# Attention prologue moved among the last experts, a bank of its own for the last batch, and a values' product in two key blocks

## The chip, the cores and the metric

One core of one Trainium2 chip runs one program. The metric is the device time of one execution in microseconds (us), lower is better. In a trace, engines are PE (matrix products), DVE, ACT and POOL; PE loads weights as instructions of their own (PEld).

## What is computed

Four stages on x of 4 batches of 256 tokens and 128 features, each with a layer norm and a residual:

```python
x = x + xattn0(layernorm(x), ctx, ...)   # trilinear attention, context to query and query to context
x = x + experts(layernorm(x), Wg, W1, W2, W3)   # 8 experts, top 2, silu(x W1) * (x W2) W3
x = x + xattn1(layernorm(x), ctx, Wq, Wk, Wv, Wo, bo)   # 16 heads of 8, softmax over 256 keys
x = x + ffn1(layernorm(x), kernel, bias)   # scaled, rounded to float8, product, bfloat16 bias
```

The change touches the third stage, and the second where the third now reaches into it.

## The kernel before

Every engine has a hand-written order of instructions, and semaphores in the dictionary S join them: `then_inc` counts up, `wait_ge` holds the engine, and everything behind it, until the count is there. PSUM has eight banks bk[0] to bk[7] of 128 partitions by 512 fp32 numbers.

**Start.** `project_keys` (L1056) multiplies wk with ctxT, a half of the tokens at a time, into banks 2 and 3, after the values' projection (L1051) and just ahead of the experts; ACT copies the result over ctxT (L402). PE's wait for cv is at L1003.

**Experts.** 16 units (8 experts for each half of the tokens). PE: `up(n)` (12 products of 512 columns, lines 933 to 935, into banks 0 to 3), then `down(n - 2)` (L1110, into bank 4 or 5). ACT: `gates` (L409). DVE: `hidden` (L756) and `weigh(n - 2)` (L768), which adds the weighted result to xs. The first half of xs is complete after unit 7; its layer norm for the attention is `sum_moments` on DVE in unit 9, POOL's `deviation_and_shift` (lines 237 to 276), four `third_scaled` on ACT (L413) in units 10 and 11, `turn("ln3", ...)` on PE (L941) after down() of unit 12, `third_turned` on ACT (L427), and `project_queries(0)` (L1117) at the head of unit 13. ACT and DVE split the queries into a high and a low part (L432, L779).

**Attention.** 16 groups of 4 heads, m = 4 b + g for batch b. For a group, `pick_group` (L1127) spreads queries and keys of its heads over 32-row strips, ACT's `stacked` (L438) moves them to stk; `scores(m, r)` (L1144), one strip r at a time, gives head r's scores; DVE's `maxima` (L789) takes the row maxima into negm; `turn_maxima` (L1152) transposes these; DVE's `shifted` (L798) puts them into qa; `shifted_scores` (L1164) computes the scores once more, transposed, with the shift, into banks 3 to 6; ACT's `exps` (L446) writes probs; `outputs` (L1177) multiplies them with values and ones into bank 7; ACT's `o_copy` (L454) takes it to heads_out. Per batch, `turn_outputs` (L1186), DVE's `normalise` (L806, L808), `turn_normalised` (L1193), ACT's `turned_out` (L458), `output_layer` (L1199) and DVE's `add_attention` (L815) follow, spread over the groups of the next batch by `bank7_used` and `bank7_free`, which also hold what has to be read from bank 7 before outputs overwrites it. `keep_warm` (L947) are products of the identity with itself whose result nobody reads.

On PE a group runs: `turn_maxima(m)`, `bank7_used(m)`, `scores(m+1, 1)`, `pick_group(m+3)`, `shifted_scores(m)`, `scores(m+1, 2)`, `scores(m+1, 3)`, `bank7_free(m)`, `outputs(m-1)`, `scores(m+2, 0)`. On DVE: `maxima(m+1, 0)`, `shifted(m)`, `maxima(m+1, 1)`, extras, `maxima(m+1, 2)`, extras, `maxima(m+1, 3)`. In groups 0 and 1 the extras are the moments of the second half of xs (L563, L566), in group 13 both halves' `normalise`. The stretch between experts and groups is:

```python
down(UNITS - 2); scores(0, 0); scores(0, 1); down(UNITS - 1); pick_group(2)
scores(0, 2); keep_warm(7, 4); scores(0, 3); keep_warm(7, 3); scores(1, 0)
```

SP issues loads and the three stores alone; no DMA is touched.

## Time and profile before

| | us |
|---|---|
| median of 3 runs | 216.92 |
| lowest, highest | 216.85, 217.7 |
| profiled execution, its own time | 218.05 |
| span of its trace | 216.3 |

The profile says 87% busy for PE, 64% for DVE, 48% for ACT and 17% for POOL, and a mean granted clock of 0.945. A row of the timeline gives start and length; instructions of one line that follow each other are merged (xN), and square brackets say how long the engine was idle before and who released it. A row of the chain gives start, length and what the chain ran through. Matmul records overlap, so a merged length is a little longer than the share of the chain.

### The profile page before, as it was taken

Reading aid. Unit: us, or ns where it says so; the run is one execution under the profiler, and the core shown is the slowest. Engines: PE = TensorE matmul, PEld = TensorE weight load, DVE = VectorE, ACT = ScalarE, POOL = GpSimd, SP = SyncE. Lnnn points to the kernel's source line nnn. Section 1 sums busy time; section 2 is a strip of 40 time slices with the busy share of each in tenths; the row PEclk is TensorE's granted clock in tenths of the full one; section 3 lists DMA queues with packets and bytes.
Section 4 is the critical chain, followed back from the end, with each engine's and each line's share of the span. In section 5 each row is a group of like instructions: output and inputs, shape, how many; then the busy total and the mean of one; then the engine's idle time right before and its main releaser. Section 6 shows DMA issues by size and latency. Waiting matters only on the chain.

```text
span 216.3 us, 3877 instructions
## 1 busy us (share of the span) xinstructions
PE 188.8 (87%) x1386; PEld 146.3 (68%) x1386; DVE 139.3 (64%) x404; ACT 103.9 (48%) x184; POOL 36.7 (17%) x52
## 2 busy tenths in 40 slices
PE   5599799999999999998999999799999998789221
PEld 4289498779798888996789886456666665554110
DVE  2559758666467647553546778477777876554684
ACT  2247467535422232533233146887577666345333
POOL 3623374624000000300000005200000000003400
PEclk9999999999999999999999999999999999655955
DMA  6992000000000000000000000000000000000002
GB/s 205 387 397 92 5 0 2 0 3 0 0 5 0 0 0 3 0 0 0 3 0 0 2 3 0 0 3 0 5 0 3 0 5 0 0 3 2 0 0 97
DMA packets 3330, 6.61 MB, mean 31 GB/s; under 512 B 880, under 2 KB 2160, under 8 KB 3056
## 3 DMA queue, kind: packets, MB, share of 16 engines
q1 hardware_dynamic: 1440, 5.51, 6.7%
q10 hardware_dynamic: 1872, 0.87, 1.4%
q8 instruction: 11, 0.18, 0.3%
q14 instruction: 7, 0.06, 0.1%
HBM read 5.84 MB, written 0.52 MB: 29 GB/s over the span
## 4 chain that ended last, share of the span: by engine, by line
PE 74%; DVE 11%; issue 5%; ACT 5%; ACTq 3%; POOL 1%; DVEq 0%
PE banks L1110 13%; PE bank L1144 9%; PE bank L1177 8%; PE bank L933 5%; PE bank L935 5%; PE bank L934 5%; DVE negm L789 4%; PE bank L947 3%; PE bank L1152 3%; PE banks L934 2%; PE banks L933 2%; PE banks L935 2%; ACTq L328 2%; PE bank L1186 2%; PE bank L1127 2%
## 5 line engine op out<-in xcount | busy, mean ns | idle before, releaser
L789 DVE TENSOR_REDUCE negm<-bank 128x2 f32<-128x512 f32 x64 | 43.0, 689 | 18.9 <-PE bank L1144 18.7
L446 ACT ACTIVATE raw<-banks 128x1024 f32<-128x1024 f32 x32 | 31.0, 1021 | 21.4 <-PE banks L1164 21.4
L409 ACT ACTIVATE att<-bank 128x512 f32<-128x512 f32 x32 | 19.1, 598 | 38.5 <-PE bank L935 25.6
L1144 PE MATMUL bank<-stk 32*128 32x256 f32 x128 | 29.9, 319 | 3.9 <-DVE negm L789 3.3
L1144 PEld LDWEIGHTS bank<-stk 32*128 32x128 f32 x128 | 19.4, 191 | 15.9 <-issue 12.8
L768 DVE SCALAR_TENSOR_TENSOR xs<-banks,rw,xs 128x128 f32<-128x128 f32 x64 | 18.0, 345 | 6.0 <-PE banks L1110 5.8
L1110 PEld LDWEIGHTS banks<-raw,attT 128*128 128x128 f32 x176 | 21.3, 191 | 0.9
L1110 PE MATMUL banks<-raw,attT 128*128 128x128 f32 x176 | 21.5, 275 | 0.0
L1177 PE MATMUL bank<-raw,vones 128*32 128x256 f32 x256 | 19.9, 433 | 1.1 <-DVE ao L808 1.0
L933 PE MATMUL bank<-xT,w 128*128 128x512 f32 x48 | 20.6, 428 | 0.0
L237 POOL TENSOR_SCALAR vpe<-mv 128x4 f32<-128x4 f32 (+1 forms) x9 | 2.4, 266 | 97.7 <-DVE mv L566 97.6
L935 PE MATMUL bank<-xT,w 128*128 128x512 f32 x48 | 18.8, 392 | 0.0
L934 PE MATMUL bank<-xT,w 128*128 128x512 f32 x48 | 18.8, 391 | 0.0
L438 ACT ACTIVATE stk<-bank,const 128x512 fp32r<-128x512 f32 x16 | 11.2, 699 | 8.8 <-PE bank L1127 8.8
L756 DVE TENSOR_TENSOR attT<-att,bank 128x512 f32<-128x512 f32 x11 | 7.5, 683 | 10.3 <-ACT att L409 10.3
L1164 PE MATMUL banks<-qa,stk 32*128 32x256 f32 x128 | 13.5, 335 | 0.5 <-DVE qa L798 0.5
L1177 PEld LDWEIGHTS bank<-raw,vones 128*32 128x32 f32 x256 | 8.4, 119 | 6.8 <-issue 1.9
L756 DVE TENSOR_TENSOR attT<-att,banks 128x512 f32<-128x512 f32 x11 | 7.6, 688 | 7.2 <-ACT att L409 7.2
L263 POOL TENSOR_TENSOR w<-raw,w 128x512 fp32r<-128x512 f32 x8 | 10.1, 1286 | 6.6 <-ACT w L341 5.2
L933 PEld LDWEIGHTS bank<-xT,w 128*128 128x128 f32 x48 | 9.0, 188 | 2.7 <-DVE xT L697 0.5
L1164 PEld LDWEIGHTS banks<-qa,stk 32*128 32x128 f32 x128 | 10.0, 198 | 0.9 <-DVE qa L798 0.9
L935 PEld LDWEIGHTS bank<-xT,w 128*128 128x128 f32 x48 | 9.0, 188 | 2.1
(194 smaller groups left out, 347.6 us busy)
## 6 DMA issues: line engine op xcount, KB each, us to landing
raw<-in_w SPq DMA_DIRECT2D x1, 2048.0 KB, 10.7
raw<-in_w SPq DMA_DIRECT2D x1, 1024.0 KB, 8.5
xs<-in_x SPq DMA_DIRECT2D x2, 256.0 KB, 3.2
ctxT<-in_ctxT SPq DMA_DIRECT2D x1, 512.0 KB, 5.3
ctx<-in_ctx SPq DMA_DIRECT2D x1, 512.0 KB, 7.4
wl<-in_wl SPq DMA_DIRECT2D x1, 256.0 KB, 7.6
picks<-in_sel ACTq DMA_DIRECT2D x1, 256.0 KB, 10.9
out<-cT SPq DMA_DIRECT2D x1, 256.0 KB, 2.1
```

Of the source, the lines that this page charges most:

```text
L409: act.activation(silus[:, k, :], bk[2 * k][:, :], ACT.Silu).then_inc(S["silu_s"], 1)
L446: act.activation(probs[:, m % 2, 2 * r:2 * r + 2, :, :].rearrange("p h k q -> p (h k q)"), pair[r][:, :], ACT.Exp, scale=ATT_SCALE).then_i ...
L756: dve.tensor_tensor(hid[n % 3][:, k, :], silus[:, k, :], bk[2 * k + 1][:, :], ALU.mult)\
L768: ins = dve.scalar_tensor_tensor(xs[:, tile, :], bk[4 + n % 2][:, t * P:(t + 1) * P], rw[:, tile, e:e + 1], xs[:, tile, :], ALU.mult, ALU.add)
L789: dve.tensor_reduce(negm[:, m % 2, :, c0:c0 + 1].rearrange("p t c -> p (t c)"), bk[score_bank(m, r)][:, :].rearrange("p (t k) -> p t k", t ...
L933: pe.matmul(out, w[0], x[0], start=start, stop=False)
L934: pe.matmul(out, w[0], x[1], start=False, stop=False)
L935: return pe.matmul(out, w[1], x[0], start=False, stop=stop)
L1110: ins = pe.matmul(bk[4 + p][:, rows], hid[n % 3][:, k, rows], w3raw[:, e, k * P:(k + 1) * P], start=t == 0 and k == 0, stop=t == TPH - 1 a ...
L1144: ins = pe.matmul(bk[score_bank(m, r)][:, t * SEQ:(t + 1) * SEQ], stk[rows, m % G, t * P:(t + 1) * P], stk[rows, m % G, SEQ:2 * SEQ], star ...
L1164: ins = pe.matmul(bk[3 + j][:, t * SEQ:(t + 1) * SEQ], stk[rows, g, SEQ + t * P:SEQ + (t + 1) * P], qa[rows, m % 2, :], start=True, stop=T ...
L1177: ins = pe.matmul(bk[bank][QUAD * j:QUAD * (j + 1), SEQ:2 * SEQ], vones[:, t, (m % G) * HPG + j, :], probs[:, m % 2, j, t, :], start=t == ...
```

## The change

- The first key product goes between context_to_query(1) and the wait for cv; both keys land in kraw, which shares x3T's memory, and ACT copies the first ahead of the values.
- The turn, queries and selections of the first groups go one unit earlier, and behind up(); group 0's scores stand around down() in units 14 and 15, all in bank 6, DVE's maxima around weigh(). The last down() goes into group 0, into bank 7; the one before it uses bank 0. DVE's last two weigh() go into group 0.
- ACT's third_scaled of unit 10 and 11 join in unit 10; those of group 2 go ahead of its exponentials. DVE's moments of groups 0 and 1 join in group 1.
- 15 keep_warm products go from units and group 0, four come into the last group.
- outputs is split by key block, with scores(m+2, 0) between the two.
- Batch 2's turns, layer and normalising use bank 0; its second turn goes behind the values' product of group 13, its output layer into group 14.

```diff
@@ -31,7 +31,7 @@
 SHIFT_ROW = 24
-WARMED = (0, 1, 2, 2 * G - 1, 3 * G - 1)
+WARMED = (1, 2, 2 * G - 1, 3 * G - 1)
@@ -140,6 +140,7 @@
 x3T = sb("x3T", [P, TOK])
+kraw = x3T
@@ -179,11 +180,17 @@
 def score_bank(m, r):
     if m == 0:
-        return 2 - r % 2
+        return 6
...
 def turn_bank(b, t):
-    return 0 if t == 0 and b >= BATCH - 2 else 7
+    return 0 if b == BATCH - 2 or (t == 0 and b == BATCH - 1) else 7
...
+def layer_bank(b):
+    return 0 if b == BATCH - 2 else 7
...
+def y_bank(n):
+    return {UNITS - 2: 0, UNITS - 1: 7}.get(n, 4 + n % 2)
@@ -277,7 +284,7 @@
     pool.wait_ge(S["k_hi"], 1)
-    pool.tensor_tensor(kx[:, 1, :], ctxT[:, :], plain(kx[:, 0, :]), ALU.subtract).then_inc(S["k_lo"], 1)
+    pool.tensor_tensor(kx[:, 1, :], kraw[:, :], plain(kx[:, 0, :]), ALU.subtract).then_inc(S["k_lo"], 1)
...
     def values(b, first):
@@ -394,12 +401,15 @@
+    def keys_out(h):
+        act.wait_ge(S["k_ps"], h + 1)
+        act.copy(kraw[:, h * HALF:(h + 1) * HALF], bk[2 + h][:, :]).then_inc(S["k_out"], 1)
...
+    keys_out(0)
...
     normed_hi(0)
-    for h in range(2):
-        act.wait_ge(S["k_ps"], h + 1)
-        act.copy(ctxT[:, h * HALF:(h + 1) * HALF], bk[2 + h][:, :]).then_inc(S["k_out"], 1)
+    keys_out(1)
     def gates(n, first):
@@ -455,7 +465,7 @@
     def turned_out(b):
         act.wait_ge(S["aoT_ps"], b + 1)
-        act.copy(aoT[:, :], bk[7][:, 0:SEQ]).then_inc(S["aoT_ev"], 1)
+        act.copy(aoT[:, :], bk[layer_bank(b)][:, 0:SEQ]).then_inc(S["aoT_ev"], 1)
     def act_group(m):
@@ -465,27 +475,27 @@
             turned_out(b - 1)
+        if m == 2:
+            for t in range(*HALVES[1]):
+                third_scaled(t)
...
         if m >= 1:
-            o_copy(m - 1, 0 if m == GROUPS - 1 else 7)
+            o_copy(m - 1)
...
             stacked(m + 3)
-        if m == 2:
-            for t in range(*HALVES[1]):
-                third_scaled(t)
...
             logits_out(1)
-        if n == UNITS - 3:
+        gates(n, n == 0)
+        if n == UNITS - 4:
             queries_hi(0)
-        if n >= UNITS - 2:
-            stacked(n - UNITS + 2, 7)
-        gates(n, n == 0)
+        if n >= UNITS - 3:
+            stacked(n - UNITS + 3, 7)
         if n == 2:
-            act.copy(kx[:, 0, :], ctxT[:, :]).then_inc(S["k_hi"], 1)
+            act.copy(kx[:, 0, :], kraw[:, :]).then_inc(S["k_hi"], 1)
@@ -493,13 +503,12 @@
             gap_tanh(n // 5)
-        if n in (E + 2, E + 3):
-            for k in range(HB):
-                third_scaled(HB * (n - E - 2) + k)
-        if n == E + 4:
+        if n == E + 2:
+            for t in range(*HALVES[0]):
+                third_scaled(t)
+        if n == E + 3:
...
     act.activation(spare[:, :], const[:, C_ZERO:C_ZERO + 1], ACT.Exp)
-    stacked(2)
@@ -765,7 +774,7 @@
             tile = h * TPH + t
-            ins = dve.scalar_tensor_tensor(xs[:, tile, :], bk[4 + n % 2][:, t * P:(t + 1) * P],
+            ins = dve.scalar_tensor_tensor(xs[:, tile, :], bk[y_bank(n)][:, t * P:(t + 1) * P],
@@ -813,7 +822,7 @@
         dve.tensor_tensor(xs[:, tiles, :], xs[:, tiles, :],
-                          bk[7][:, 0:SEQ].rearrange("p (t d) -> p t d", t=TPB), ALU.add)\
+                          bk[layer_bank(b)][:, 0:SEQ].rearrange("p (t d) -> p t d", t=TPB), ALU.add)\
...
     def dve_group(m):
@@ -824,6 +833,8 @@
             maxima(m + 1, 1)
+        if m == 0:
+            weigh(UNITS - 2)
@@ -834,15 +845,18 @@
             maxima(m + 1, 2)
-        if m in (0, 1):
-            sum_moments((TPH + TPB * m, TPH + TPB * (m + 1)))
+        if m == 0:
+            weigh(UNITS - 1)
+        if m == 1:
+            sum_moments(HALVES[1])
+        if more:
+            maxima(m + 1, 3)
...
             normalise(b - 1, 1)
-        if more:
-            maxima(m + 1, 3)
+        if m == GROUPS - 2:
+            add_attention(b - 1, slice(TPB * (b - 1), TPB * b))
...
             moments(4, CHUNKS[0], lambda t: dve.wait_ge(S["x3_s"], t // TPB + 1))
-            add_attention(b - 1, slice(TPB * (b - 1), TPB * b))
@@ -853,17 +867,18 @@
             routing(n // 5)
-        if n == UNITS - 3:
+        if n == UNITS - 4:
             queries_lo(0)
+        if n == UNITS - 2:
+            dve.wait_ge(S["setup"], 1)
+        if n >= UNITS - 2:
+            maxima(0, 2 * (n - UNITS + 2))
...
             weigh(n - 2)
+        if n >= UNITS - 2:
+            maxima(0, 2 * (n - UNITS + 2) + 1)
...
             sum_moments(HALVES[0])
-    weigh(UNITS - 2)
-    dve.wait_ge(S["setup"], 1)
-    maxima(0, 0, 1)
-    weigh(UNITS - 1)
-    maxima(0, 2, 3)
@@ -1000,6 +1015,12 @@
     context_to_query(1)
+    def project_keys(h):
+        ins = pe.matmul(bk[2 + h][:, :], wk[:, :], ctxT[:, h * HALF:(h + 1) * HALF], start=True, stop=True)
+        ins.then_inc(S["k_ps"], 1)
...
+    pe.wait_ge(S["ld_att"], 7 * 16)
+    project_keys(0)
@@ -1053,14 +1074,7 @@
-    def project_keys(h):
-        if h == 0:
-            pe.wait_ge(S["aT_ev2"], BATCH - 1)
-        ins = pe.matmul(bk[2 + h][:, :], wk[:, :], ctxT[:, h * HALF:(h + 1) * HALF], start=True, stop=True)
-        ins.then_inc(S["k_ps"], 1)
...
-    for h in range(2):
-        project_keys(h)
+    project_keys(1)
     def logits(h):
@@ -1099,15 +1113,17 @@
     def down(n):
-        e, p = n % E, n % 2
+        e = n % E
...
         pe.wait_ge(S["hid_s"], HB * (n + 1))
-        if n > 1:
+        if 1 < n < UNITS - 2:
             pe.wait_ge(S["y_w"], n - 1)
+        if n == UNITS - 1:
+            pe.wait_ge(S["stack_s"], 3)
...
             for k in range(HB):
-                ins = pe.matmul(bk[4 + p][:, rows], hid[n % 3][:, k, rows], w3raw[:, e, k * P:(k + 1) * P],
+                ins = pe.matmul(bk[y_bank(n)][:, rows], hid[n % 3][:, k, rows], w3raw[:, e, k * P:(k + 1) * P],
@@ -1121,6 +1137,8 @@
         pe.wait_ge(S["stack_s"], m)
+        if m == 3:
+            pe.wait_ge(S["y_w"], UNITS - 1)
@@ -1131,14 +1149,14 @@
     def scores(m, r):
         pe.wait_ge(S["stack_s"], m + 1)
-        if r == 0 and m > 0:
+        if m == 0:
+            pe.wait_ge(S["s1_max"], r)
+        elif r == 0:
             pe.wait_ge(S["s1_max"], 4 * m - 1)
-        elif r == 2 and m > 0:
+        elif r == 2:
             pe.wait_ge(S["qa_s"], m)
-        elif r == 3 or (r == 1 and m > 0):
+        else:
             pe.wait_ge(S["s1_max"], 4 * m + (r + 1) // 2)
-        elif r == 2:
-            pe.wait_ge(S["s1_max"], 1)
@@ -1155,6 +1173,8 @@
     def shifted_scores(m):
         pe.wait_ge(S["qa_s"], m + 1)
+        if m == 0:
+            pe.wait_ge(S["y_w"], UNITS - 2)
@@ -1167,17 +1187,18 @@
-    def outputs(m, bank=7):
+    def outputs(m, bank=7, blocks=range(TPB)):
...
             pe.wait_ge(S["o_ev"], m)
-        for j in range(HPG):
-            for t in range(TPB):
+        for t in blocks:
+            for j in range(HPG):
...
                                 start=t == 0, stop=t == TPB - 1, tile_position=(0, QUAD * j))
-        ins.then_inc(S["pv_ps"], 1)
+        if blocks[-1] == TPB - 1:
+            ins.then_inc(S["pv_ps"], 1)
     def turn_outputs(b, t):
@@ -1190,13 +1211,13 @@
     def turn_normalised(b):
...
         for t in range(TPB):
-            ins = pe.transpose(bk[7][:, t * P:(t + 1) * P], ao[:, t, :], ident)
+            ins = pe.transpose(bk[layer_bank(b)][:, t * P:(t + 1) * P], ao[:, t, :], ident)
...
     def output_layer(b):
...
         for t in range(TPB):
-            ins = pe.matmul(bk[7][:, t * P:(t + 1) * P], aoT[:, t * P:(t + 1) * P], wo[:, :],
+            ins = pe.matmul(bk[layer_bank(b)][:, t * P:(t + 1) * P], aoT[:, t * P:(t + 1) * P], wo[:, :],
@@ -1207,36 +1228,39 @@
             turn("ln3", "x3T_ps", 7, 1)
+        if m == 1:
+            pe.wait_ge(S["y_w"], UNITS)
...
             project_queries(1)
-        if g == 0 and b >= 2:
+        if g == 0 and 2 <= b:
             output_layer(b - 2)
+        if m == 3 * G + 1:
+            pe.wait_ge(S["stack_s"], GROUPS)
         if b >= 1 and g == 1:
-            if b == BATCH - 1:
-                pe.wait_ge(S["stack_s"], GROUPS)
             turn_outputs(b - 1, 0)
-            if b == BATCH - 1:
-                turn_outputs(b - 1, 1)
...
         if m in TURNED_AT:
+            pe.wait_ge(S["ao_s"], TPB * b)
...
     def bank7_free(m):
         b, g = m // G, m % G
+        if m == 1:
+            pe.wait_ge(S["y_w"], UNITS)
...
             pe.wait_ge(S["x3_s"], b - 1)
-        if b >= 1 and g == 1:
-            pe.wait_ge(S["ao_s"], TPB * (b - 1) + (1 if b < BATCH - 1 else TPB))
+        if 1 <= b < BATCH - 1 and g == 1:
+            pe.wait_ge(S["ao_s"], TPB * (b - 1) + 1)
...
             pe.wait_ge(S["ao_s"], TPB * b)
-        if m in TURNED_AT:
+        if 1 <= b < BATCH - 1 and g == 3:
...
     def pe_group(m):
@@ -1246,25 +1270,31 @@
             scores(m + 1, 1)
-        if m + 3 < GROUPS:
+        if 0 < m < GROUPS - 3:
...
         shifted_scores(m)
-        if final:
-            pe.wait_ge(S["o_ev"], m - 1)
-            output_layer(BATCH - 2)
-            outputs(m - 1, 0)
+        if m == 0:
+            down(UNITS - 1)
...
             if m == 0:
-                keep_warm(7, 2)
+                pick_group(3)
             scores(m + 1, 3)
-        if m == 0:
-            keep_warm(7, 4)
-        if m >= 1 and not final:
+        if m >= 1:
             bank7_free(m)
-            outputs(m - 1)
+            outputs(m - 1, 7, (0,))
...
             scores(m + 2, 0)
+        if m >= 1:
+            outputs(m - 1, 7, (1,))
+        if m == 3 * G + 1:
+            pe.wait_ge(S["ao_s"], TPB * (BATCH - 2) + 1)
+            turn_outputs(BATCH - 2, 1)
+        if m == 3 * G + 2:
+            pe.wait_ge(S["aoT_ev"], BATCH - 1)
+            output_layer(BATCH - 2)
+        if final:
+            keep_warm(2, 4)
@@ -1278,40 +1308,34 @@
             pe.wait_ge(S["xT_lo"], 2)
-        if n == UNITS - 3:
-            pe.wait_ge(S["route_s"], 18)
-            project_queries(0)
-        if n == UNITS - 2:
-            pe.wait_ge(S["pick_s"], 1)
-            pe.wait_ge(S["k_lo"], 1)
-        if n >= UNITS - 2:
-            pick_group(n - UNITS + 2, 7)
...
             logits_turned(1)
+        if n == UNITS - 5:
+            turn("ln3", "x3T_ps", 6, 0)
+        if n == UNITS - 4:
+            pe.wait_ge(S["route_s"], 18)
+            project_queries(0)
+        if n == UNITS - 3:
+            pe.wait_ge(S["pick_s"], 1)
+            pe.wait_ge(S["k_lo"], 1)
+        if n >= UNITS - 3:
+            pick_group(n - UNITS + 3, 7)
+        if n >= UNITS - 2:
+            scores(0, 2 * (n - UNITS + 2))
...
             logits(1)
-        if n == E + 4:
-            turn("ln3", "x3T_ps", 6, 0)
+        if n >= UNITS - 2:
+            scores(0, 2 * (n - UNITS + 2) + 1)
+    pe.wait_ge(S["hid_s"], HB * UNITS)
+    scores(1, 0)
     down(UNITS - 2)
-    pe.wait_ge(S["hid_s"], HB * UNITS)
-    for r in range(2):
-        scores(0, r)
-    down(UNITS - 1)
-    pick_group(2)
-    scores(0, 2)
-    pe.wait_ge(S["stack_s"], 2)
-    keep_warm(7, 4)
-    scores(0, 3)
-    keep_warm(7, 3)
-    scores(1, 0)
-    pe.wait_ge(S["setup"], 1)
...
     outputs(GROUPS - 1, 1)
+    pe.wait_ge(S["x3_s"], BATCH - 1)
     turn_outputs(BATCH - 1, 0)
-    pe.wait_ge(S["x3_s"], BATCH - 1)
...
     output_layer(BATCH - 1)
```

## Rows read from the trace of the kernel before

**Rows 1.** The page: its span, and the granted clock and DMA share in 40 slices.

```profile
span 216.3 us, 3877 instructions
PEclk9999999999999999999999999999999999655955
DMA  6992000000000000000000000000000000000002
```

**Rows 2.** The page's costliest groups (operation, shapes, busy, mean, idle before).

```profile
L789 DVE TENSOR_REDUCE negm<-bank 128x2 f32<-128x512 f32 x64 | 43.0, 689 | 18.9 <-PE bank L1144 18.7
L446 ACT ACTIVATE raw<-banks 128x1024 f32<-128x1024 f32 x32 | 31.0, 1021 | 21.4 <-PE banks L1164 21.4
```

**Rows 3.** Timeline of an attention group: start, length, engine and line, idle before.

```profile
157.76 1.09 PE L1177 MATMUL bank<-raw,vones 128*32 128x256 f32 x16
158.78 0.50 PE L1144 MATMUL bank<-stk 32*128 32x256 f32 x2
159.22 0.44 PE L1152 MATMUL bank<-const,negm 128*128 128x128 f32 x2
159.22 0.69 ACT L438 ACTIVATE stk<-bank,const 128x512 fp32r<-128x512 f32 x1
159.49 0.61 PE L1199 MATMUL bank<-wo,aoT 128*128 128x128 f32 x4
160.16 0.35 PE L1144 MATMUL bank<-stk 32*128 32x256 f32 x1
161.51 0.47 PE L1144 MATMUL bank<-stk 32*128 32x256 f32 x2 [0.26 <-DVE negm L789]
```

**Rows 4.** Timeline and chain of waits around the key products.

```profile
23.98 0.60 PE L1005 MATMUL banks<-const,cv 128*4 128x128 f32 x4 [1.31 <-DVE cv L638]
...
37.90 0.69 DVE L697 TENSOR_TENSOR xT<-banks,xT 128x512 fp32r<-128x512 f32 x1
...
38.10 0.86 PE banks L1059 x2
```

**Rows 5.** Timeline of experts 12 and 13.

```profile
97.34 1.13 DVE L768 SCALAR_TENSOR_TENSOR xs<-banks,rw,xs 128x128 f32<-128x128 f32 x4 [0.47 <-PE banks L1110]
98.50 1.10 PE L1117 MATMUL bank<-x3T,wq 128*128 128x512 f32 x2 [0.77 <-ACT x3T L427]
...
104.61 0.47 PE L1127 MATMUL bank<-qx,pick 32*128 32x256 f32 x2 [0.46 <-DVE qx L779]
```

**Rows 6.** Groups by line on PE from 120 to 129 us; chain of waits there.

```profile
L947 PE MATMUL bank<-const 128*128 128x128 f32 x34 | 5.2, 287 | 0.0
...
120.58 1.09 PE bank L947 x8
```

**Rows 7.** Timelines of DVE, POOL and PE, and the chain, up to group 3.

```profile
131.03 0.30 DVE L566 BATCH_NORM_AGGREGATE mv<-stats 128x2 f32<-128x6 f32 x2
...
133.26 0.20 POOL L276 TENSOR_TENSOR nmr<-nmr,rstd 128x4 f32<-128x4 f32 x1
...
136.96 1.53 ACT xn L413 x4
...
137.49 1.38 PE L941 MATMUL bank<-const,xn 128*128 128x128 f32 x4 [0.90 <-ACT xn L413]
```

**Rows 8.** Timeline and chain of waits of the last batch.

```profile
180.95 1.07 PE L1186 MATMUL bank<-const,heads_out 128*128 128x128 f32 x8 [0.36 <-issue]
184.80 1.19 PE L1177 MATMUL bank<-raw,vones 128*32 128x256 f32 x16 [1.02 <-DVE ao L808]
...
190.12 1.89 PE bank L1177 x16
195.10 3.67 PE bank L1177 x32
```

**Rows 9.** Stretches: PE, PEld, DVE, ACT, POOL busy (instructions), PEclk, DMA share, GB/s.

```profile
134.50:138.00 3.50, 2.60 (x24) 1.31 (x23) 2.07 (x4) 3.50 (x8) 0.31 (x1) 1.00 0.00 0
182.00:185.50 3.50, 1.85 (x29) 1.27 (x30) 2.80 (x7) 1.94 (x2) 0.00 (x0) 1.00 0.00 0
```

## The prediction, made before the change was run

> **What bounds the kernel now.** I read the page first: busy times, slices and PEclk. The granted clock is full for 34 of 40 slices and falls near the end [rows 1]. Then the chain of waits, which shows TensorE nearly everywhere, and last the timelines of the places where the chain names something other than a dense PE stream.
>
> Two regimes. Through the experts (39 to 117 us) PE runs without a gap. In the attention groups one group takes some 4.15 us, in a ring. The second scores product of group m+1 starts at 160.16, its maxima on DVE take 0.69 [rows 2], the fourth product starts at 161.51 [rows 3], and then PE alone: that product (0.47), the values' product (from 157.76 to 158.78 in the group before, 1.02), the next first scores (158.78 to 159.22, 0.44), the maxima's transposes (0.37 of chain time) and one filler on bank 7 (from 159.49, 0.45 of chain time) [rows 3]. From 160.16 to 161.51 is 1.35, most of it work. So PE's own work is about 3.7 of 4.15, and what is merely reordered inside the ring brings little. The reader should look for what is outside it:
>
> - Keys and start of the experts: PE idles 1.31 before the row of maxima at 23.98, while both key products lie at 37.24 to 38.96, just ahead of the experts, which could start when DVE's low half is written, at 37.90 + 0.69 = 38.59 [rows 4].
> - Experts 12 and 13: PE stands 0.77 for the copy of x3T and 0.46 for the queries' low half [rows 5].
> - Groups 0 and 1: between 120 and 129 PE runs 34 keep-warm products, 5.2 us busy in that row [rows 6], in the places where it would wait.
> - Group 3: the second half's turn waits for four scalings on ACT and ends at 138.87 [rows 7]. The transpose of the maxima ended at 136.59.
> - Last batch: the values' product of group 12 waits 1.02 for normalising on DVE, since both halves were turned ahead of it and one of them is in its bank. Then the granted clock falls: the same 16 instructions of the values' product take 1.19, then 1.89, and the last 32 take 3.67 [rows 8], against 1.02 before. In the 3.5 us around the stall PE was busy 1.85; in group 3's stall 2.60 of 3.5, and the clock stayed [rows 9].
>
> **The sum, part by part** (chain time; minus is saved).
>
> 1. First key product (0.86) moves into the 1.31 hole at 22.7. Its cover is the wait for cv; without it, it would cost 0.86. It also moves the wait for the attention weights forward; the DMA row shows the last traffic in the fourth slice of 5.4 us, so by 21.6 [rows 1], before the hole. ACT's copy of it comes ahead of the values' copies, in idle time. The experts then start at 38.64 and not 38.96, DVE being late next: **-0.3**.
>
> 2. Turn, queries and selection one expert earlier, and behind up() instead of ahead of it: ACT's copies and DVE's subtraction pass under down() and the next up(). The two idles (0.77, 0.46) and the slow start of L1117 (1.10 for what L1059 does in 0.86) [rows 4, 5] go: **-1.45**. The four scalings now stand together on ACT in expert 10 and delay the next gate by some 0.2; the hidden layer has more slack than that, so nothing.
>
> 3. From expert 14 to group 3's second scores product (138.86). Keep-warms: 34 records fall to 4, which is 30 x 0.136 = **-4.1** (8 of them take 1.09 on the chain) [rows 6]. The last down() moves from ahead of group 0's third scores into group 0: neutral by itself. Added: eight more places where row-tiled products stand alone between full-array ones. What such a switch costs no row isolates. The nearest rows: a pair of scores takes 0.50 behind the values' product and 0.47 elsewhere [rows 3], and a turn or a selection behind down() overlaps its end or not, by up to 0.2. I take 0.1 each, between the two: **+0.8** (0 to 1.6). Overlap lost in group 0, whose second and third scores and selection shared PE with the shifted scores: **+0.75** (bounds 0 and 1.4, three pairs of 0.47 standing alone). New wait: DVE now does both last weigh() (1.13 each [rows 5]) inside group 0, between its maxima. The fourth maxima of group 1 ends about 5.9 + 0.7 after group 0's transposes begin, PE is done at 5.4: **+1.2** (0 to 1.9). In group 1 the four moments (two pairs of 0.6) stand together ahead of the fourth maxima, and turn_maxima(2) waits: **+0.75** (0 to 1.2). Who waits behind it on PE is the whole queue. Group 3: the scalings run ahead of group 2's exponentials, not behind them. They wait for POOL, which needs 133.46 - 131.33 = 2.1 behind the moments [rows 7], and push the exponentials (two of 1.02 [rows 2]) by 1.0; o_copy(1) follows them and PE waits some 0.9 for it, where it waited 1.9 before: **-0.9** (0 to -1.9). Rest of my timeline +0.35. Together **-1.1** (-3 to +0.8). Of the DVE moments' delay nothing else comes free: group 2 hides it.
>
> 4. The ring, groups 4 to 12. Splitting the values' product puts the next first scores 0.48 earlier, so DVE's first maxima no longer hold the second scores: they begin 0.06 behind the filler's end (159.49 + 0.61), where back-to-back groups overlap by 0.07 (158.78 against 157.76 + 1.09), so 0.13 is that wait. Against it stands a second switch, 0.1 and a little. And o_copy, hence stacked(m+3), now ends some 0.4 later; stacked ends at 159.91 [rows 3] with PE's selection just behind 160.16, so the selection slips by some 0.2 into the hole of 0.26 that follows (idle of the row at 161.51). Per group -0.1 to +0.15; I take 0, over nine groups -0.9 to +1.4: **0**. Here the row shows weights of L1144 loading only once the values' product is through: its first matmul and load begin together at 158.78, and two need 0.50 where 0.47 is the rule [rows 3]. The Trainium skill (TensorE: Matmul & The Clock Gate, Part 3, "The mechanism") says a weight load overlaps running matmuls only where the row group differs. The values' product fills all 128 rows, so by it each extra block is an exposed load, which speaks against this split, and over 14 groups the sum would be some 1.7 worse than mine.
>
> 5. Last batch, from group 13's transposes (180.95 - 0.36 - 0.37 = 180.22) to the end of the last values' product (195.10 + 3.67 = 198.77): 18.55 [rows 8]. After, at full clock, from X: transposes 0.37; wait for stacked(15), longer than the 0.36 by the later o_copy, 0.88; four transposes 0.5; to the fourth scores 1.35; 0.47; half values 0.51; wait for the third maxima behind one normalising 0.27; scores 0.43; 0.51; other four transposes 0.5: X+5.8. Before it was 6.5 with the stall. Then DVE, which has nothing else, normalises the second half (0.55, about half of the 1.02 that two of them held PE) ahead of the first maxima (0.69) + 0.15: second scores at X+7.25; +1.35; 0.47; values 1.02; output layer 0.45: X+10.55. Then 0.37, qa and shifted scores 1.05 (an estimate, below the 1.35 of a ring, which has more in it), two exponentials 1.94, values 1.02 behind the last: X+15.15. **-3.4**. At full clock both ways the old order would be shorter by 0.8; nearly all of the gain is the clock, which I take to stay up since the longest PE hole is now about 0.9 with 2.3 us busy in 3.5, as in group 3's case that kept it.
>
> 6. Behind this, DVE and POOL work on the final layer stays as it was: their slack in the last groups shrinks. 0.
>
> Sum: -0.3 - 1.45 - 1.1 - 0 - 3.4 = **-6.3**. The profiled execution took 218.05 (span 216.3, 1.75 around it) and would take 211.8. It lies 1.1 above the median of 216.92; part of that may be how long the low clock lasted. Against the median: 216.92 - 6.3 = 210.6.
>
> **Rivals.**
>
> B. The clock falls in the last batch all the same. For: little of groups 13 and 14 is values' product, and it once fell there. Against: no hole of 1 us. Price: the pieces at half clock against those at full, 0.87 for each values' product, 0.3 for scores, 0.25 for transposes, and 1.8 at the end, 4.2: **214.8**.
>
> C. The clock falls in groups 0 to 3, slower. Place: turn_maxima(1), waiting 1.2 for DVE with the keep-warms gone, then 0.75 and 0.9 in the next two. A ring's 3.7 of PE work becomes by the ratios of rows 8 (1.89 to 1.02) about 6.3: +2.2 a group. It decides from the third group on, since 6.3 / 2.2 = 2.9. With five groups at half clock: **221.6** (216.92 - 6.3 + 11). Against: at 21.5 to 25 and in group 3 the clock survived holes over 1 us [rows 7, 9].
>
> D. The split's second switch costs PE its 0.12 in each group, and the earlier maxima bring nothing, PE being the bound: 14 x 0.12 = 1.7 more: **212.3**. For: the rows of a ring [rows 3]. Against: the 0.13 that the second scores wait there. The rule of the Trainium skill's TensorE page named in 4 leads here. A kindred rival is that selections wait on stacked() by more than the hole hides, 0.2 x 9 = 1.8, the same time.
>
> E. It does not do what it says: groups 0 to 2 are bound by DVE (weigh, moments), so that removed keep-warms only become waits. Term 3 is then +0.8 and with B the sum is -0.35: **216.6**.
>
> **Chances.** Forecast 0.53, B 0.17, D 0.16, C 0.09, E 0.05. The range of A is 210.6 with -1.9 / +1.9 from terms 3 and 4; to D and B it reaches 215.2, below it 207.8. About 0.5% (1.1 us) is what a measurement of this kernel tells from no change. Faster 0.86, same 0.05, slower 0.09.
>
> **What would show it.** Right: L1059's first product at 22.7; up(0) at 38.6; no idle ahead of L1117 and L1127 in the experts; turn_maxima(1) near 125.3 behind a DVE wait; group 3's second scores at 136; steady rings of 4.15; PEclk 9 until the last slices; values' product of 1.02 in groups 13 and 14, split in two of 0.5. Wrong: PEclk below 9 in slices 22 to 34, rings of 4.3 or more, a stall on stk ahead of L1127, or DVE as releaser of L1152 in every group.

## The result, and the profile after

The changed kernel takes 227.41 us in the median of 4 runs (224.15 to 247.13), the kernel before 217.17. By the comparison, which leaves disturbed runs out, the ratio is 1.037 with a 95% interval of 1.028 to 1.046: slower. The spread of the changed kernel is itself a finding: over its four runs the mean granted clock went from 0.898 (span 222.3) down to 0.766 (span 245.3). The profiled execution took 228.54, span 226.8.

The page of the changed kernel, span and granted clock in 40 slices; before, the clock was full up to slice 34 [rows 1]:

```profile
span 226.8 us, 3850 instructions
PEclk9999999999999999999998555599999995556955
```

The clock is now low twice before the tail: from 123.2 to 147.1 and from 188.0 to 208.5. PE's timeline where it first falls (start, length, engine and line, idle before and its releaser), and two stretches of the windows (length, PE busy and four other engines' busy time, PEclk, DMA share, GB/s):

```profile
121.83 0.47 PE L1162 MATMUL bank<-stk 32*128 32x256 f32 x2 [0.40 <-DVE negm L798]
123.37 0.69 PE L1170 MATMUL bank<-const,negm 128*128 128x128 f32 x2 [1.07 <-DVE negm L798]
...
119.70:123.20 3.50, 2.20 (x18) 1.70 (x16) 2.22 (x7) 1.50 (x2) 0.00 (x0) 1.00 0.01 2
130.00:137.00 7.00, 7.00 (x46) 4.43 (x44) 3.10 (x5) 4.52 (x9) 2.96 (x4) 0.50 0.00 0
```

turn_maxima(1) (L1170) comes at 123.37, 4.5 earlier than before, but behind a hole of 1.07 us in which PE waits for DVE's maxima, and the clock falls in that hole. From 130 to 137 PE shows no idle time at all, at half clock. The start of turn_maxima(m), read from each trace, makes a table by group:

| stretch, us | before | after |
|---|---|---|
| start of turn_maxima(1) | 127.9 | 123.4 |
| groups 1 to 4 | 18.7 | 26.5 |
| groups 5 to 12 | 33.6 | 37.1 |
| group 13's transposes to the last values' product's end | 18.6 | 22.3 |
| from there to the span's end | 17.5 | 17.6 |

That is -4.5 + 7.8 + 3.5 + 3.7 + 0.1, the 10.5 between the spans but for rounding. Groups 5 to 12, the third line, are at full clock, where a group takes 4.54 to 4.76 in place of 4.14 to 4.36 [rows 3]. One such group:

```profile
149.88 0.44 PE L1170 MATMUL bank<-const,negm 128*128 128x128 f32 x2
150.02 0.37 ACT L464 COPY heads_out<-bank 128x256 f32<-128x256 f32 x1 [0.67 <-PE bank L1197]
150.53 0.63 PE L1207 MATMUL bank<-const,heads_out 128*128 128x128 f32 x4 [0.22 <-ACT heads_out L464]
151.09 0.38 PE L1162 MATMUL bank<-stk 32*128 32x256 f32 x1
...
152.47 0.47 PE L1162 MATMUL bank<-stk 32*128 32x256 f32 x2 [0.38 <-DVE negm L798]
152.87 0.64 PE L1197 MATMUL bank<-raw,vones 128*32 128x256 f32 x8
153.56 0.47 PE L1162 MATMUL bank<-stk 32*128 32x256 f32 x2
153.95 0.64 PE L1197 MATMUL bank<-raw,vones 128*32 128x256 f32 x8
154.52 0.44 PE L1170 MATMUL bank<-const,negm 128*128 128x128 f32 x2
```

Two things are new. The filler (L1207; the products that bank7_used puts behind the transposes) waits for ACT's o_copy (L464): it begins 0.65 behind the transposes of the maxima, 0.27 before (159.22 to 159.49 [rows 3]). And from the fourth scores (152.47) to the next transposes (154.52) is 2.05, where it was 1.85 before (161.51 to 163.36).

### The profile page after: what moved, and what is told of

Its sections match the earlier page's. It is cut to its first block, busy times and chain, and to the rows that moved or that the text cites. A ratio compares the mean times of both kernels' runs of the same rounds, so it can differ in the third digit from the quotient of the medians.

```text
span 226.8 us, 3850 instructions
## 1 busy us (share of the span) xinstructions
PE 200.6 (88%) x1364; PEld 147.1 (65%) x1364; DVE 140.3 (62%) x404; ACT 104.4 (46%) x184; POOL 36.8 (16%) x52
## 4 chain that ended last, share of the span: by engine, by line
PE 73%; DVE 13%; issue 5%; ACT 3%; DMA 3%; POOL 1%; SPq 1%; DVEq 0%; ACTq 0%
PE banks L1126 11%; PE bank L1197 11%; PE bank L1162 10%; PE bank L948 5%; PE bank L950 5%; PE bank L949 5%; DVE negm L798 4%; DMA ctx<-in_ctx 3%; PE bank L962 2%; PE bank L1207 2%; PE banks L948 2%; PE banks L949 2%; PE banks L950 2%; PE bank L1126 2%; PE banks L1184 2%
## 5 line engine op out<-in xcount | busy, mean ns | idle before, releaser
L798 DVE TENSOR_REDUCE negm<-bank 128x2 f32<-128x512 f32 x60 | 40.3, 689 | 21.7 <-PE bank L1162 21.1
L1162 PE MATMUL bank<-stk 32*128 32x256 f32 x120 | 32.4, 364 | 3.8 <-DVE negm L798 3.5
L1162 PEld LDWEIGHTS bank<-stk 32*128 32x128 f32 x120 | 21.8, 228 | 17.9 <-issue 16.9
L1197 PE MATMUL bank<-raw,vones 128*32 128x256 f32 x256 | 25.5, 488 | 0.0
L777 DVE SCALAR_TENSOR_TENSOR xs<-banks,rw,xs 128x128 f32<-128x128 f32 x56 | 15.8, 345 | 7.8 <-PE banks L1126 7.7
L1126 PEld LDWEIGHTS banks<-raw,attT 128*128 128x128 f32 x160 | 19.2, 192 | 1.2 <-issue 0.5
L1126 PE MATMUL banks<-raw,attT 128*128 128x128 f32 x160 | 19.7, 276 | 0.0
L1184 PE MATMUL banks<-qa,stk 32*128 32x256 f32 x128 | 16.0, 380 | 0.6 <-DVE qa L807 0.5
L464 ACT COPY heads_out<-bank 128x256 f32<-128x256 f32 x16 | 6.0, 373 | 16.0 <-PE bank L1197 16.0
L1184 PEld LDWEIGHTS banks<-qa,stk 32*128 32x128 f32 x128 | 12.0, 235 | 1.2 <-DVE qa L807 1.2
L270 POOL TENSOR_TENSOR w<-raw,w 128x512 fp32r<-128x512 f32 x8 | 10.2, 1291 | 6.6 <-ACT w L348 5.2
```

What stands on the lines that cost most here:

```text
L777: ins = dve.scalar_tensor_tensor(xs[:, tile, :], bk[y_bank(n)][:, t * P:(t + 1) * P], rw[:, tile, e:e + 1], xs[:, tile, :], ALU.mult, ALU.add)
L798: dve.tensor_reduce(negm[:, m % 2, :, c0:c0 + 1].rearrange("p t c -> p (t c)"), bk[score_bank(m, r)][:, :].rearrange("p (t k) -> p t k", t ...
L1126: ins = pe.matmul(bk[y_bank(n)][:, rows], hid[n % 3][:, k, rows], w3raw[:, e, k * P:(k + 1) * P], start=t == 0 and k == 0, stop=t == TPH - ...
L1162: ins = pe.matmul(bk[score_bank(m, r)][:, t * SEQ:(t + 1) * SEQ], stk[rows, m % G, t * P:(t + 1) * P], stk[rows, m % G, SEQ:2 * SEQ], star ...
L1184: ins = pe.matmul(bk[3 + j][:, t * SEQ:(t + 1) * SEQ], stk[rows, g, SEQ + t * P:SEQ + (t + 1) * P], qa[rows, m % 2, :], start=True, stop=T ...
L1197: ins = pe.matmul(bk[bank][QUAD * j:QUAD * (j + 1), SEQ:2 * SEQ], vones[:, t, (m % G) * HPG + j, :], probs[:, m % 2, j, t, :], start=t == ...
```

## Experiments

**Fill the hole (e1), join the product (e2), both (e3), split the old kernel (e4).**

e1, in pe_group, behind scores(m+2, 0):

```diff
+                if m == 0:
+                    pe.wait_ge(S["stack_s"], G)
+                    keep_warm(0, 8)
```

> The changed kernel with eight identity products (16 records) in bank 0 behind group 0's last product, once stacked(3) is read, so that PE works where it waited 1.07 us for the maxima. Theory 1 (the low clock of groups 1 to 4 comes from that hole): the clock stays full through groups 1 to 4, turn_maxima(1) comes at 123.4 to 123.7, groups 1 and 2 take 4.6 to 5 us in place of 6.6 and 6.8, and the time falls by 7 to 9 to 218 to 220. Rival (the clock falls for another reason, such as the smaller share of full-array work, or the last down() in group 0): it falls all the same within some 4 us, time within 2 of 227.

e2:

```diff
-                    outputs(m - 1, 7, (0,))
+                    outputs(m - 1)
                 if m + 2 < GROUPS:
                     scores(m + 2, 0)
-                if m >= 1:
-                    outputs(m - 1, 7, (1,))
```

> The changed kernel with the values' product in one piece again, ahead of scores(m+2, 0). Theory 2 (with the split, o_copy ends later than the transposes of the maxima, and bank7_used makes PE wait for it): groups at full clock return from 4.58 to 4.15, and nothing is idle ahead of the filler; the low clock in groups 1 to 4 stays; time 222 to 225. Rival (the second switch between row and column tiles costs the 0.43): the same 4.15, but the trace of the changed kernel would show no idle PE ahead of the filler. Rival (the ring grew by the later stacked(m+3)): also 4.15, idle ahead of L1145 there. Rival (DVE's order): stays 4.58.

e3 is e1 and e2 together:

```diff
-                    outputs(m - 1, 7, (0,))
+                    outputs(m - 1)
                 if m + 2 < GROUPS:
                     scores(m + 2, 0)
-                if m >= 1:
-                    outputs(m - 1, 7, (1,))
+                if m == 0:
+                    pe.wait_ge(S["stack_s"], G)
+                    keep_warm(0, 8)
```

> Both edits. Theories 1 and 2 add: about 227.4 - 8 - 5 = 214 to 215, below the kernel before, with groups 1 to 12 at 4.15 but for group 3. If the clock falls for another reason: as e2, 222 to 225.

e4, the kernel before with outputs() split as in the change:

```diff
-                    outputs(m - 1)
+                    outputs(m - 1, 7, (0,))
                 if m + 2 < GROUPS:
                     scores(m + 2, 0)
+                if m >= 1 and not final:
+                    outputs(m - 1, 7, (1,))
```

> The kernel before with the split alone. Theory 2: each group from 2 on takes 0.4 more, 12 x 0.43 = 5: 221 to 223, with the clock full until the last batch. Rival (the cost comes only together with the bank changes): within 1 of 217.

Measured, beside the kernel before at 217.83:

| | median (range), us | ratio to before |
|---|---|---|
| e1 fill | 217.76 (214.95 to 241.96) | 0.9985 [0.993, 1.004] |
| e2 whole | 211.63 (208.71 to 215.52) | medians 0.972, no interval |
| e3 both | 212.58 (210.02 to 225.03) | 0.971 [0.954, 0.987] |
| e4 split alone | 226.14 (225.69 to 228.09) | 1.040 [1.024, 1.056] |

e1's page, and the stretch around the former hole:

```profile
PEclk9859999999999999999999999999999999969955
...
119.70:123.20 3.50, 3.10 (x27) 2.67 (x26) 2.22 (x8) 2.44 (x3) 0.00 (x0) 1.00 0.01 2
130.00:137.00 7.00, 6.26 (x66) 4.16 (x65) 4.48 (x8) 5.93 (x11) 3.20 (x5) 1.00 0.00 0
```

The clock stays full there, groups 1 and 2 take 4.27 and 4.38 in place of 6.58 and 6.82, groups 1 to 4 together 18.7 as before the change, and the kernel is level with the one before. So it is this hole that costs the clock here: in both traces that have it open (the changed kernel, e2) the clock falls at or just behind it, and in all seven that have it filled (e1, e3, e5, e6, e9, e10, e12) it is full until 130 us at least. It isn't the only place: three of ten runs of e1 still took 238 to 242, and where the clock fell in these isn't known.

e2 is the surprise. I had expected 222 to 225, thinking that the low clock of groups 1 to 4 would stay as long as it did. It fell behind the same hole (which ends at 123.94), at 124.5, but came back after 6.8 us, not 23.9:

```profile
PEclk9999999999999999999999995999999999999855
...
175.19 1.07 PE L1197 MATMUL bank<-raw,vones 128*32 128x256 f32 x16
```

Its groups at full clock take 4.11 to 4.12 (4.36 with keep-warms), against 4.14 (4.36) before. All four runs of e2 lie below the lowest of the kernel before, 216.21. e4 says the same from the other side: the split alone costs the kernel before some 4%, 4.54 to 4.76 a group. That is above my 221 to 223, since the clock did not stay full: group 3 took 7.75 in place of 5.87. The hole ahead of the second half's turn was 1.19 us there, 0.90 before, and the clock fell at 139.5, 1.9 behind its end. e3 came out below its 214 to 215; eight products took more time than the hole had (group 0: 6.98 in place of 6.23), and in its profiled execution the clock fell at 133.2, in group 3's hole:

```profile
133.28 1.11 PE L956 MATMUL bank<-const,xn 128*128 128x128 f32 x4 [0.85 <-ACT heads_out L464]
```

**What in the split costs 0.43 a group (e5, e6, e9, e11).** Both e5 and e6 start from e1. e5 puts the filler, and its wait for o_copy, behind the second scores; e6 keeps the new order of the matmuls but nothing between the blocks:

```diff
# e5
-                if not final:
-                    bank7_used(m)
                 if more:
                     scores(m + 1, 1)
+                if not final:
+                    bank7_used(m)
# e6
                     outputs(m - 1, 7, (0,))
+                    outputs(m - 1, 7, (1,))
                 if m + 2 < GROUPS:
                     scores(m + 2, 0)
-                if m >= 1:
-                    outputs(m - 1, 7, (1,))
```

> The kernel of e1_warm (split kept, keep-warms in group 0's hole) with the filler on bank 7, and its wait for o_copy, behind scores(m+1, 1) instead of ahead of it. Theory 2 (of the 0.43 that a split ring takes more, some 0.3 is PE's wait for o_copy ahead of the filler, 0.12 the second switch): groups with the clock full take 4.2 to 4.3. Rival (it is the switches alone): 4.55 to 4.6 as in e1.

> The kernel of e1_warm with both key blocks in a row, so the new order of the 16 matmuls (key block outside, head inside) without the scores product in the middle. Theory 2: 4.12 to 4.15 a group at full clock, as with the old order. Rival (the order itself, or the four accumulations open at once, is slow): over 4.3.

e6 took 211.53, in one run, with 4.11 to 4.12 a group: the order itself is free. e5 said nothing on the ring: its clock fell at 130.2 and stayed low for 92 us, 246.11 in all (one run). I repeated it with the move in groups 5 to 12 only (e9):

```diff
+                late = G < m <= 3 * G
-                if not final:
+                if not final and not late:
                     bank7_used(m)
                 if more:
                     scores(m + 1, 1)
+                if late:
+                    bank7_used(m)
```

> As e5, but the filler and its wait for o_copy go behind scores(m+1, 1) only in groups 5 to 12, so that the early groups are those of e1_warm and the clock should be full where the rings are measured. Theory 2: those groups take 4.25 to 4.35 at full clock, against 4.58 in e1. Rival (the second switch alone makes the 0.43, o_copy nothing): 4.55 to 4.6.

Inconclusive again: low from 142.8 for 75 us, 239.07 (one run). What the two do show is that the clock falls without such a hole too: in the 8 us ahead of the fall PE's longest idle stretch was 0.50 in e5 and 0.40 in e9. e4's clock had been full there in its trace, so e11 makes the move on e4, in groups 6 to 12:

```diff
+                late = G + 1 < m <= 3 * G
-                if not final:
+                if not final and not late:
                     bank7_used(m)
                 if more:
                     scores(m + 1, 1)
+                if late:
+                    bank7_used(m)
```

> The kernel of e4_split_before (before with the split alone; its clock was full from 146 to 190 us) with the filler and its wait for o_copy behind scores(m+1, 1) in groups 6 to 12. Theory 2: at full clock these groups take 4.25 to 4.35, against 4.54 to 4.76 in e4. Rival (the second switch makes all of the 0.43): unchanged, 4.54 to 4.76. If the clock falls there, the test says nothing again.

Now (one run, 225.34) the clock was full from 147.7 to 192.1, and the groups took 4.28 to 4.30 (4.71 and 4.72 where keep-warms and a turn are among what moved) against 4.54 to 4.64 and 4.76 in e4. Its timeline, where ACT's copy (L454) no longer stands ahead of the second scores at 160.09:

```profile
159.71 0.44 PE L1152 MATMUL bank<-const,negm 128*128 128x128 f32 x2
159.85 0.37 ACT L454 COPY heads_out<-bank 128x256 f32<-128x256 f32 x1
160.09 0.49 PE L1144 MATMUL bank<-stk 32*128 32x256 f32 x2
```

So of the 0.43 some 0.3 is the wait for o_copy. The rest, 0.14 against the kernel before, is what stays when that wait is covered; the second switch of tiles is its likely cause, but no run isolates it. The changed kernel's own rows say the same: 0.3 more from the transposes to the fourth scores (2.59 against 2.29), 0.2 more from there on (2.05 against 1.85).

**Keep-warms and last batch alone, on the kernel before (e7, e8).** e7 takes the 15 keep-warm products out:

```diff
-WARMED = (0, 1, 2, 2 * G - 1, 3 * G - 1)
+WARMED = (1, 2, 2 * G - 1, 3 * G - 1)
...
-                    if m == 0:
-                        keep_warm(7, 2)
...
-                if m == 0:
-                    keep_warm(7, 4)
...
-            keep_warm(7, 4)
             scores(0, 3)
-            keep_warm(7, 3)
```

> The kernel before without its 15 keep-warm products between the last experts and group 1. Theory 1 (keep-warms hold the clock over holes there, and only that): the clock falls between 118 and 130 us in most executions, groups 1 to 3 take 6 us or more, time 222 to 228. Rival (the clock there hangs on the hole that weigh and moments make in the changed kernel, and the kernel before has none such): clock full, and since PE waits for DVE in the same places, time 215 to 217.

232.29 in the median (220.4 to 243.22), above my 222 to 228; the fastest of the four runs is 3.0 above the kernel before's median (217.35). Its trace, span 233.1, has the clock low from 122.1 for 10.2 us, and from 139.2 for 51. The holes are the one of 1.01 us shown here and group 3's of 0.90; the clock fell 2.1 and 2.2 behind their ends:

```profile
120.03 0.47 PE L1144 MATMUL bank<-stk 32*128 32x256 f32 x2 [1.01 <-DVE negm L789]
...
PEclk9889999999999999999995695555555569956955
...
160.00:175.00 15.00, 14.98 (x104) 10.12 (x104) 7.91 (x14) 8.12 (x11) 0.00 (x0) 0.50 0.00 1
```

So keep-warms were worth far more than the time they took. And the low clock can last in groups with an unsplit product too: the split isn't needed for it.

e8 makes the change's last batch on the kernel before: bank 0 for batch 2, its second turn behind group 13's product, the output layer in group 14, and DVE's order and the four keep-warm products of the last group as in the change. Two cuts of it:

```diff
                     turn_outputs(b - 1, 0)
-                    if b == BATCH - 1:
-                        turn_outputs(b - 1, 1)
...
+                if m == 3 * G + 1:
+                    pe.wait_ge(S["ao_s"], TPB * (BATCH - 2) + 1)
+                    turn_outputs(BATCH - 2, 1)
+                if m == 3 * G + 2:
+                    pe.wait_ge(S["aoT_ev"], BATCH - 1)
+                    output_layer(BATCH - 2)
+                if final:
+                    keep_warm(2, 4)
```

> The kernel before with the change's last batch alone (batch 2 through bank 0, its second turn behind group 13's values' product, four keep-warms in the last group). Step 5 of the prediction: from group 13's transposes of the maxima to the last values' product 15.2 in place of 18.55, clock full there, time 217.2 - 3.4 = 213.8 (213 to 215). Rival (the clock falls there all the same): 216 to 218.

215.11 in the median (213.43 to 217.8), ratio 0.988 [0.979, 0.997]: two runs at 213.4 and 213.7, as forecast, two at 216.5 and 217.8, as by the rival. The chain of waits in its trace, from group 13's transposes to the last values' product, to be held against [rows 8]:

```profile
179.79 0.37 PE bank L1156 x2
180.16 0.36 issue
180.52 0.63 PE bank L1190 x4
...
182.92 1.02 PE bank L1181 x16
...
188.14 1.02 PE bank L1181 x16
...
191.16 1.02 PE bank L1181 x16
192.18 1.09 PE bank L951 x8
193.27 1.09 PE bank L1181 x16
```

From 179.79 to 194.36 is 14.6, not 18.6, with every values' product at 1.02 to 1.09. This is a trace of the 213.7 run. Of the two runs above 216 only the mean clock is known, 0.934 and 0.956 against 0.970; where it fell isn't.

**A version that beats both (e10, e12).** e10 is e3 with four products, not eight, in group 0's hole. e12 adds two in group 13 and two in group 14, ahead of the waits there:

```diff
# e10, against e3
-                    keep_warm(0, 8)
+                    keep_warm(0, 4)
# e12, against e10
-WARMED = (1, 2, 2 * G - 1, 3 * G - 1)
+WARMED = (1, 2, 2 * G - 1, 3 * G - 1, 3 * G + 1, 3 * G + 2)
```

> The changed kernel with the values' product in one piece and four keep-warm products (8 records, 0.9 us) in group 0's hole of 1.07 us, half of those of e3, which made group 0 longer by 0.75. Theory: group 0 takes 6.25 as in e2, groups 1 and 2 4.3 and 4.0 as in e3, and the time is 209 to 212, the fastest of all. Rival (the clock falls as often as in e2 or e3, one hole later): 211 to 213, the same as e2.

> The kernel of e10_warm_four with two keep-warm products each in groups 13 and 14, ahead of PE's waits there for stacked(15) and for the normalised half. Theory (e10's slower executions, 215 against 209, are those in which the clock falls in the last batch, at 178 us in its trace): fewer of them, median 209 to 211. Rival (the clock falls as often): median 213 as e10, with at most 0.3 added for the products.

e10: 213.09 (209.03 to 215.08), 0.966 [0.959, 0.972]. Group 0 took 6.23, groups 1 and 2 4.33 and 4.02, as expected. The time was not: its trace, of a run of 214.98, has the clock falling at 177.9, in group 13, and three of six runs took about 215. e12: 209.18 (208.76 to 211.38), 0.966 [0.961, 0.970], all six runs within 2.6. Against e10's ratio it shows no gain; the median is 3.9 lower, and 8.2 below the kernel before (217.35). That the four products keep the clock in the last batch is likely (none of six runs near 215 in place of three, and the clock full there in its trace), but six runs each, on different chips, don't settle it. Its page:

```profile
span 207.0 us, 3867 instructions
PE 182.0 (88%) x1380; PEld 141.4 (68%) x1380; DVE 140.7 (68%) x404; ACT 103.6 (50%) x184; POOL 36.9 (18%) x52
PEclk9999999999999999999999999999999999999955
```

## Why the prediction was wrong

The prediction was -6.3 (210.6); the change gave +10. Two steps failed. One is step 4, the ring: it put the split of the values' product at 0 (-0.1 to +0.15 a group), and it costs 0.43 a group, mostly PE's wait for o_copy. The other is the clock, which step 3 put at nothing when it took out the keep-warms, and which step 5 took to stay up in the last batch; it was at half for 23.9 us from group 0's hole on and for 20.5 us from group 13 on. Between -6.3 and the +10.5 of the spans lie 16.8 us: 3.5 of these came in groups 5 to 12 (the split, at full clock), 6.2 before group 5 and 7.1 in the last batch (where the clock was low). By the prediction's steps:

1. **First key product: -0.3 predicted, -0.05 measured.** It went into the hole, whose idle shrank from 1.31 to 0.46. From the row of maxima to the experts' second matmul is 15.00 against 15.05 before. The key products had nearly all been under DVE's xT work already: the prediction took the start of the experts, 38.96, from the chain, which puts it at the modelled end of the key product, while PE's timeline of the kernel before has it at 38.64:

```profile
37.94 1.02 PE L1059 MATMUL banks<-ctxT,wk 128*128 128x512 f32 x2
38.64 0.54 PE L933 MATMUL bank<-xT,w 128*128 128x512 f32 x1
```

   (The profiled executions also differ by 0.8 in when cv is ready, which isn't the change's.)

2. **Turn, queries, selections: -1.45 predicted, -1.5 measured** (up(14)'s second product starts at 103.27 against 105.60, less that 0.8 and step 1's 0.05). No idle is left ahead of L1133 and L1145. Right.

3. **Experts to group 3: -1.1 predicted.** Measured at full clock, e12's group 4 begins 5.0 earlier than before; less 0.5 of start-up and the 1.55 of steps 1 and 2, that is -2.9, at the edge of my bounds, with four keep-warms added. The wait before turn_maxima(1) was 1.07, forecast 1.2. What was too high lies on both sides of turn_maxima(0): that came at 117.1, or 117.9 without the 0.8 of start-up, where the forecast 125.3 less 5.9 + 0.7 gives 118.7, and group 0 took 6.2 where it gives 6.6. The 0.8 for switches and the 0.75 for lost overlap stand there; which of them was too high no run shows. What the step lacks is the clock: groups 1 to 4 took 18.7 with the hole filled (e1) and 26.5 with it open.

4. **The ring: 0 predicted, 0.43 a group measured, 0.3 of it the wait for o_copy.** I had a term for the switch (0.12) and the later stacked(). What I missed is that bank7_used waits for o_ev ahead of every filler. Before, scores(m+2, 0) and turn_maxima hid the copy; the split puts the end of the product directly ahead of turn_maxima, and the wait is bared. My own text names the later o_copy and follows it to stk, not to the nearest waiter: the step left out one queue. e11 parts the wait from the rest, and e6 clears the new order. The rule of the Trainium skill (TensorE: Matmul & The Clock Gate, Part 3, "The mechanism"), that a weight load overlaps running matmuls only where the row group differs, pointed the right way: halves of 0.57 and 0.61 on the chain where the whole takes 1.00 agree with exposed loads at each change of tiles. With at most 0.14 to 0.2 a group it was the smaller part.

5. **Last batch: 15.15 predicted against 18.55; at full clock 14.6 measured in e8 and 14.45 in e2** (176.69 to 191.14 in its chain), values' products at 1.02. (From X+10.55 on the terms named add up to 14.93, not 15.15.) So the size was right, if the clock stays. That it stays was wrong for the changed kernel, where the clock fell at 188.0, in group 13, 184.50 to 188.00 having 2.47 us of PE work, and the stretch took 22.3. There PE waited some 0.8 for stacked(15), as forecast (0.88); with the whole product it is 0.33 (e2). Nor is it the split alone: of the seven traces that bring a full clock into group 13 with this last batch and no more fillers, five lose it before the batch's last values' product (the changed kernel, e1, e3, e6, e10) and two keep it (e2, e8). The forecast's "no hole of 1 us" did not guard it; in e10 the longest idle stretch ahead of the fall was 0.63. That is rival B, which got 0.17.

6. **Tail: 0**, 17.6 against 17.5. Right.

Rival C named the place (turn_maxima(1), waiting for DVE with the keep-warms gone) and, with five groups, 221.6. It got 0.09. Its price doesn't follow from what it names: 3.7 us by the ratio of 1.89 to 1.02 is 6.9, not 6.3; measured, the four low groups took 26.5 in place of 18.7, 2.0 more each. I gave it so little because the clock had survived a hole of 1.31 at 22.7 [rows 4] and one of 0.90 in group 3 [rows 7], which the prediction rounds up to "over 1 us"; that was evidence from one execution. E (0.05) had holes without the clock (its sum comes to -0.15, not -0.35). What none of them had is that B, C and D (the dearer ring) come together.

Steps 1 to 3, 5 and 6 without the split are e2: 211.63, against 210.6 forecast for the whole. That nearness is partly luck: step 3 gave 1.8 more than forecast, and e2's 6.8 us of low clock took 1.3 of it back (groups 1 to 4 at 19.3 against 18.0 in e12). Why the low clock lasts longer with the split (23.9 against 6.8 us, 75 and 92 in e9 and e5) stays open: e7 has 51 us of it without a split and e3 27, so it is no clean rule, and one trace per kernel doesn't tell chance from cause.

## What to carry to other kernels

When an instruction is moved or split, list everything that waits for its end, nearest first, and check that each still has cover; a reorder that frees one engine's wait can bare another's. Products that look idle but hold the clock are to be removed only with the hole that they filled; a hole of about 1 us that costs nothing in one trace may cost 10 us in another (group 3's in e3 against e6), so look at several runs before calling a clock safe. Test the parts of a combined edit alone: here the split by itself turned -6.2 (e2) into +10.

## What the runs showed of the hardware

- After a fall of the clock, PE busy 7.00 of 7 us, or 14.98 of 15, did not bring it back at once; the low stretches before the tail lasted from 3.4 (e1) to 92 us (e5).
- The same timetable can keep or lose it: group 3's hole of 0.85 us lost it in e3's trace and kept it in e6's.
- It falls in a hole (123.2 in the changed kernel), up to 2.2 us behind one (e7, e4), or with no idle stretch over 0.50 and 0.40 in the 8 us before (e5, e9).
- At half clock a group is bound by PE alone (busy 14.98 of 15 us in e7, 15.00 in e5 and e9), at 6.4 us with a whole product (e7) and 6.7 with a split one and the filler moved (e9, e5), against 4.14 and 4.28 (e11) at full clock.
- Four accumulations open at once in one bank, key block outside and head inside, cost nothing (e6, 4.12 a group).
